# Attention stage rewritten as one uniform body of 16 units, with the score mask added on TensorE and one maximum per unit

## What is computed

```python
qkv = ln(x) @ qkv_w + qkv_b                 # 16 heads of 16
dist = q_pos[:, None] - k_pos[None, :]
allowed = (dist > 0) & (dist <= 128) & (k_pos >= 0)      # a window of 128 keys
scores = where(allowed, q @ k.T * 0.25, -1e9)
local = softmax(scores) @ v
remote = latent_attention(ln(x)) @ rout_w + rout_b       # 64 pooled latents, 4 heads
gate = sigmoid(local @ gl_w + remote_h @ gr_w)           # per head
mixed = gate * local + (1 - gate) * remote_h
x = x + ln(mixed @ out_w + out_b)                        # then the experts' layer on ln(x)
```

## Time and profile before

| what | value |
|---|---|
| median of 3 runs | 2890.73 us (2880.72 to 2892.46) |
| the profiled execution's own time | 2857.07 us |
| its span, first to last instruction | 2855.3 us |
| PE busy | 2078.1 us, 73% |
| DVE busy | 1371.9 us, 48% |
| ACT busy | 909.4 us, 32% |
| POOL busy | 739.7 us, 26% |
| mean granted TensorE clock | 0.80 of full speed |

### The profile page before, as it was taken

The page is one execution under the profiler, slowest core; times in us unless marked ns, Lnnn a source line. Parts: engine busy times, 40 slices in busy tenths (PEclk is TensorE's granted clock), DMA queues, the critical chain, the costliest instruction groups (busy, mean ns, idle before and its releaser), DMA issues. The chain is left out here.

```text
span 2855.3 us, 45682 instructions
## 1 busy us (share of the span) xinstructions
PE 2078.1 (73%) x12978; PEld 1583.8 (55%) x12979; DVE 1371.9 (48%) x3448; ACT 909.4 (32%) x2071; POOL 739.7 (26%) x934
## 2 busy tenths in 40 slices
PE   2777776777677776777674999999879999996000
PEld 1344444444444444444452788788669999996000
DVE  3464555545564556545553444444533333333557
ACT  1323332233323332233322333333234444443001
POOL 1222333223322333223322333423300000001762
PEclk9667766777677766777676999999989999998555
DMA  3233422343144423343132322222212222223564
GB/s 61 43 54 60 74 50 48 58 66 66 38 59 59 74 45 50 54 74 61 36 52 78 103 83 73 91 77 76 77 60 67 68 67 68 68 68 120 154 202 156
DMA packets 180103, 209.74 MB, mean 73 GB/s; under 512 B 28337, under 2 KB 146482, under 8 KB 180066
## 3 DMA queue, kind: packets, MB, share of 16 engines
q1 hardware_dynamic: 167346, 174.54, 27.8%
q0 software_dynamic: 12720, 34.75, 3.7%
HBM read 88.99 MB, written 69.34 MB: 55 GB/s over the span
## 5 line engine op out<-in xcount | busy, mean ns | idle before, releaser
L489 ACT ACTIVATE prob<-bank 128x512 f32<-128x512 f32 (+1 forms) x512 | 251.1, 544 | 484.1 <-PE bank L948 482.8
L924 PE MATMUL bank<-kS,qS 48*128 48x256 f32 (+1 forms) x1024 | 179.6, 444 | 221.2 <-DVE row_max L715 221.2
L399 POOL TENSOR_SCALAR_AFFINE_SELECT prob<-prob 128x512 f32<-128x512 f32 x256 | 164.9, 644 | 672.6 <-ACT prob L489 670.9
L2020 POOL DMA_INDIRECT f_y<-yg_scratch,index x128 | 125.8, 983 | 622.8 <-DVE index L2058 578.5
L924 PEld LDWEIGHTS bank<-kS,qS 48*128 48x128 f32 x1024 | 116.0, 279 | 305.6 <-DVE row_max L715 283.0
L1827 DVE TENSOR_TENSOR b_h<-b_silu,bank 128x352 f32<-128x352 f32 x136 | 70.9, 521 | 336.8 <-ACT b_silu L1779 336.8
L963 PE MATMUL bank<-prob,v_sb 128*32 128x256 f32 (+1 forms) x2048 | 214.5, 506 | 0.0
L1353 POOL DMA_INDIRECT xg_scratch<-rows,pos x128 | 130.1, 1016 | 317.2 <-DVE pos L1508 281.2
L1881 PE MATMUL bank<-wgu_h,bxT_h 128*128 x544 | 191.2, 351 | 15.1 <-DVE bxT_l L1822 6.7
L712 DVE COPY_PREDICATED bank<-from_prev,bank 128x512 f32<-128x512 int32 x192 | 133.4, 695 | 141.0 <-PE bank L924 137.3
L715 DVE TENSOR_REDUCE row_max<-bank 128x4 f32<-128x512 f32 x256 | 176.9, 691 | 44.4 <-PE bank L924 35.0
(11 more groups left out here) (311 smaller groups left out, 5139.0 us busy)
## 6 DMA issues: line engine op xcount, KB each, us to landing
bx<-xg_scratch SPq DMA_DIRECT2D x136, 128.0 KB, 2.0
yg_scratch<-b_y SPq DMA_DIRECT2D x136, 128.0 KB, 1.7
kS<-qk_h SPq DMA_DIRECT2D x128, 128.0 KB, 5.9
qS<-qk_h SPq DMA_DIRECT2D x128, 128.0 KB, 8.0
x_in<-in_L_attn_x_dram SPq DMA_DIRECT2D x16, 512.0 KB, 3.5
kS<-qk_l SPq DMA_DIRECT2D x64, 128.0 KB, 6.8
qS<-qk_l SPq DMA_DIRECT2D x64, 128.0 KB, 8.9
x_res<-in_L_attn_x_dram SPq DMA_DIRECT2D x16, 512.0 KB, 3.5
```

Of the source, the lines that this page charges most:

```text
L399: op = e.affine_select(out=own, in_=own, compare_op=ALU.is_gt, fill=0.0, base=0, pattern=[[0, HG], [1, P]], channel_multiplier=-1)
L489: e.activation(prob[:, u % SLOTS, 2 * hp:2 * hp + 2, 0:w], src[:, :, 0:w], ACT.Exp, scale=SCALE).then_inc(keyed.frees[hp], 1)
L924: op = e.matmul(SB[:, par, hh * WIN + lo:(hh + 1) * WIN], qS[rows, tile, b * P:(b + 1) * P], kS[rows, tile, k0:k0 + w], start=(b > 0), sto ...
```

## The change

It replaces `mid` and `seam` on every engine by one `body(i, buf)` of 16 units, run for i from -2 to 17 (`live` leaves out what lies outside the 16 sequences), two bodies a loop turn:

- `window` and `maxima` still run 7 units ahead, but go on into the next sequence, so that every unit of the body has one. `weigh_values` runs three units behind across the border. `kS`, `qS` and `v_sb` get two buffers.
- Each other piece has a unit: projections of sequence i+1 in units 0 to 8, the turning, gating and mixing of i-1 in units 3 to 13, its output projection in 14 and 15, the input of i+2 in 2 to 14, the residual of i-2 in 0 to 13.
- The mask goes in by matmuls with the identity in every unit (`mask_window`, two of 512 columns); `window` adds the scores onto it. The predicated copy is gone, and the reduction runs over 1024 columns (L825), 512 in block 0.
- The banks: `PV` has one bank (4), bank 5 joins 6 and 7 (`Rounds` counts their uses).
- Local and remote outputs are copied to SBUF by ACT (`keep_local`, `keep_remote`); the gate runs once for four blocks. Two layer norms' scaling moves from DVE to ACT (`normed`; DVE makes the small `shifts`).
- `qk_h` and `qk_l` hold half of the heads: the second half waits for the DMAs of the first. ACT issues the DMA of the maxima itself, after its own write.

The diff, cut to its core, indentation shortened:

```diff
-        PV = ctx.enter_context(nc.psum_tensor("bank45", [P, 2, 512], f32))
-        banks = [t[:, k, :] for t in (SB, KB, PV) for k in range(2)]
-        psum = banks + [ctx.enter_context(nc.psum_tensor(f"bank{b}", [P, 512], f32)) for b in range(6, 8)]
+        banks = [t[:, k, :] for t in (SB, KB) for k in range(2)]
+        psum = banks + [ctx.enter_context(nc.psum_tensor(f"bank{b}", [P, 512], f32)) for b in range(4, 8)]
...
+kS = sb("kS", [P, 2, HEADS // 2, S], f32r)
+qS = sb("qS", [P, 2, HEADS // 2, S], f32r)
+v_sb = sb("v_sb", [P, 2, T, HEADS, PAD])
...
+uses = [["k0", "v0", "v2", "r1", "r2", "k1", "lT0", "xT1", "mix1", "out1"],
+        ["q0", "v1", "r0", "v3", "r3", "q1", "xT0", "mix0", "out0", "ls1"],
+        ["m1", "rkv", "a0", "a1", "m2", "a2", "a3", "rq", "m3", "lT1", "lo", "m0", "ls0"]]
+stage = {name: 1 for names in uses for name in names}
+stage.update({name: 0 for name in ("xT0", "xT1")})
+stage.update({name: 2 for name in ("m1", "m2", "m3", "lT0", "lT1", "lo")})
+stage.update({f"{kind}{n}": 3 for kind, count in (("a", T), ("r", T), ("mix", 2), ("out", 2)) for n in range(count)})
+front = Rounds(uses, stage, SEQS, [sem(f"front_full{b}") for b in range(3)], [sem(f"front_free{b}") for b in range(3)])
+FB = [psum[6], psum[7], psum[5]]
+PV = psum[4]
...
+        def body(i, buf):
+            if live(i + 2):
+                load_x(i + 2)
+            if live(i + 1):
+                spread_heads(i + 1, 1 - buf, 0)
+            if live(i - 2):
+                store_x1(i - 2)
+            if live(i + 1):
+                spread_heads(i + 1, 1 - buf, 1)
+            if live(i - 2):
+                store_xn2(i - 2)
+            if live(i - 1):
+                load_residual(i - 1)
...
+        def minus_max(i, buf, g):
             act.wait_ge(*front.filled(i, f"m{g}"))
             act.wait_ge(max_placed[g], 16 * i)
             e.activation(maxT[:, g, :], FB[front.bank(f"m{g}")][0:HG * T, 0:P], ACT.Copy,
                          scale=-1.0).then_inc(front.free(f"m{g}"), 1)
+            act.wait_ge(*front.read(i, f"m{g}"))
+            act.dma_start(qS[TERMS:P:PAIR, buf, 2 * g:2 * g + 2, :].bitcast(f32), maxT[:, g, :].bitcast(f32)).then_inc(max_placed[g], 16)
...
+        def normed(k, i, tile, ts):
+
+            act.wait_ge(shift_known[k // 2], i + 1)
+            if k == 2:
+                act.wait_ge(stored, 32 * i + 16)
+            for t in ts:
+                op = e.activation(tile[:, t, :], tile[:, t, :], ACT.Identity, scale=rstd[:, k, t:t + 1],
+                                  bias=shift[:, k // 2, t:t + 1])
+            if ts[-1] == T - 1:
+                op.then_inc((xn_ready, xn2_ready)[k // 2], 1)
...
-            own, prev = (SB[:, :, :].rearrange("p a (t w) -> p (a t) w", t=2)[:, :, k * P:(k + 1) * P] for k in (1, 0))
-            if b == 0:
-                dve.wait_ge(score_full, UNITS * i + u + 1)
-            else:
-                wait_alone(score_full, UNITS * i + u + 1)
-                e.copy_predicated(out=own, mask=from_prev[:, :].bitcast(i32).unsqueeze(1).to_broadcast([P, HG, P]), data=prev
-                                  ).then_inc(score_merged, 1)
-                dve.wait_ge(score_merged, MERGED * i + g * (T - 1) + b)
-            e.tensor_reduce(row_max[:, g, :, b], own, AX.X, ALU.max).then_inc(score_free, 1)
+            lo = P if b == 0 else 0
+            dve.wait_ge(score_full, UNITS * i + u + 1)
+            e.tensor_reduce(row_max[:, g, :, b], SB[:, :, :].rearrange("p a (t w) -> p (a t) w", t=2)[:, :, lo:WIN],
+                            AX.X, ALU.max).then_inc(score_free, 1)
...
+        def window(i, buf, u):
 
             g, b = units[u]
             if b == 0 and g % 2 == 0:
                 pe.wait_ge(spread[g // 2], SPREAD * (i + 1))
             pe.wait_ge(score_free, UNITS * i + u)
-            if b == 0:
-                for par in range(2):
-                    own = SB[:, par, :].rearrange("p (t w) -> p t w", t=2)[:, :, P:WIN]
-                    e.matmul(own, ident_r[:, :], mask_first[:, :].unsqueeze(1).to_broadcast([P, 2, P]),
-                             start=True, stop=False, skip_group_check=True)
             lo, w = (P, P) if b == 0 else (0, WIN)
+            mask = (mask_first if b == 0 else mask_window)[:, :].unsqueeze(1).to_broadcast([P, 2, w])
+            for par in range(2):
+                e.matmul(SB[:, par, :].rearrange("p (t w) -> p t w", t=2)[:, :, lo:WIN], ident_r[:, :], mask,
+                         start=True, stop=False, skip_group_check=True)
             k0 = max(b - 1, 0) * P
             for hh in range(2):
                 for par in range(2):
                     rows, tile = slice(par * PAIR, par * PAIR + TERMS), 2 * g + hh
-                    op = e.matmul(SB[:, par, hh * WIN + lo:(hh + 1) * WIN], qS[rows, tile, b * P:(b + 1) * P],
-                                  kS[rows, tile, k0:k0 + w], start=(b > 0), stop=True, skip_group_check=True)
+                    op = e.matmul(SB[:, par, hh * WIN + lo:(hh + 1) * WIN], qS[rows, buf, tile, b * P:(b + 1) * P],
+                                  kS[rows, buf, tile, k0:k0 + w], start=False, stop=True, skip_group_check=True)
             op.then_inc(score_full, 1)
...
-                pe.wait_ge(pv_read, G * i + max(g - 1, 0))
-                if g < 2:
-                    pe.wait_ge(pv_used, 2 * i)
+                pe.wait_ge(pv_read, G * i + g)
             for h in range(HG):
-                op = e.matmul(PV[h * PAD:(h + 1) * PAD, g % 2, b * P:b * P + w], v_sb[:, b, g * HG + h, :],
+                op = e.matmul(PV[h * PAD:(h + 1) * PAD, b * P:b * P + w], v_sb[:, buf, b, g * HG + h, :],
                               prob[:, u % SLOTS, 2 * (h % 2) + h // 2, 0:w], start=(b == 0), stop=(b == T - 1),
                               skip_group_check=True)
             op.then_inc(prob_used, 1)
 
...
+        def body(i, buf):
+            prev, nxt, after = i - 1, i + 1, i + 2
+            for u in range(UNITS):
+                if u + AHEAD < UNITS:
+                    if live(i):
+                        window(i, buf, u + AHEAD)
+                elif live(nxt):
+                    window(nxt, 1 - buf, u + AHEAD - UNITS)
+                if live(i):
+                    keyed_scores(i, buf, u)
+                if u >= LAG:
+                    if live(i):
+                        weigh_values(i, buf, u - LAG)
+                elif live(prev):
+                    weigh_values(prev, 1 - buf, UNITS + u - LAG)
+                if u == 0 and live(nxt):
+                    project(nxt, 1, 0)
+                if u == 1:
+                    if live(i):
+                        turn_max(i, 1)
+                    if live(nxt):
+                        project(nxt, 0, 0)
+                if u == 2 and live(nxt):
+                    values(nxt, 0)
+                    latent_pool(nxt)
+                if u == 3:
+                    if live(nxt):
+                        values(nxt, 1)
+                        values(nxt, 2)
+                    if live(prev):
+                        turn_local(prev, 0)
+                        remote(prev, 0)
+                if u == 4:
+                    if live(prev):
+                        turn_local(prev, 1)
+                        remote(prev, 1)
+                    if live(nxt):
+                        values(nxt, 3)
+                if u == 5:
+                    if live(i):
+                        turn_max(i, 2)
+                    if live(prev):
+                        turn_local(prev, 2)
+                        remote(prev, 2)
+                if u == 6:
+                    if live(prev):
+                        turn_local(prev, 3)
+                        remote(prev, 3)
+                    if live(nxt):
+                        latent_queries(nxt)
+                if u == 7 and live(nxt):
+                    project(nxt, 1, 1)
+                if u == 8 and live(nxt):
+                    project(nxt, 0, 1)
+                if u == 9 and live(i):
+                    turn_max(i, 3)
+                    turn_latents(i, 0)
+                if u == 10:
+                    if live(i):
+                        turn_latents(i, 1)
+                    if live(after):
+                        turn_x(after, 0)
+                        turn_x(after, 1)
+                if u == 11 and live(i):
+                    latent_values(i)
+                if u in (12, 13) and live(prev):
+                    turn_mix(prev, u - 12)
+                if u == 13 and live(nxt):
+                    turn_max(nxt, 0)
+                if u in (14, 15):
+                    if live(prev):
+                        project_out(prev, u - 14)
+                    if live(nxt):
+                        latent_scores(nxt, u - 14)
...
```

(41 more changed lines are left out.)

965 lines of the change are left out of this document (471 added, 494 removed).

## The result

| | before | changed |
|---|---|---|
| median of 4 runs each, us | 2887.25 | 2406.62 (2396.80 to 2411.76) |
| ratio, with its 95% interval | | 0.8332 [0.8297, 0.8367] |
| profiled execution, us | 2857.07 | 2411.76 |
| start of routing (first matmul with `ws_h`), us | 1576.9 | 1103.7 |
| from there to the end, us | 1278.4 | 1306.3 |

The kernel is 17% faster.

A forecast was written before the change was run, and what follows sets the result against it. It took the order of copy, maximum and window on one buffer as the bound. PE work of 56 us, 13% idle and clock 0.9 gave a 71 us period, 318 us saved, median 2573 us, range 2450 to 2765.

The forecast's parts named there:

- The bound: Attention loop: copy, maximum and window share one buffer, so their order sets the pace; scores wait 14.1 us for the maximum.
- The sum: Attention period from PE work, idle share and clock: 71 us, a gain of 318 us over 15 repetitions, median 2573 us.
- idle share of 13%: PE's idle part of the new body, taken from the old kernel's dense stretch: 3.72 of 28.90 us.
- clock of 0.9: Granted PE clock in the new body, from the old dense stretch's 0.91: 20% of time at 1.2 GHz.
- the first row: Old kernel's stretch while the seam projects: PE busy 25.18 of 28.90 us, clock 0.91.
- my own equation: Body period P from PE work of 56 us: 0.87P = 56 + 0.088P, giving P = 71.6.
- rival 1: Clock falls in light units 9, 12 and 13: period 80 us, 2708 us, up to 2783; chance 0.20.
- My own list of waits: Added PE waits in the body: DMAs nothing, value bank 0 to 0.2 us, about five bank waits up to 1 us each.
- rival 2: Every wait in the body is covered: period near 61 us, 2423 us; chance 0.10.
- The ends: Filling and draining of attention hold the same chains: 0 change, within 20 us either way.
- The mask part: Identity matmuls in the windows: 12 x 0.56 = 6.7 us of PE work a sequence at full clock, relieving VectorE of copies.

The follow-up runs named there:

- two maxima: The changed kernel with every maximum taken twice on VectorE, the extra one into a tile nobody reads; 2412.68 us, 0.8583 of the kernel before.
- the doubled mask: The changed kernel with each mask matmul pair issued twice, same result; 2397.57 us, 0.8530 of the kernel before.
- three maxima: The changed kernel with every maximum taken three times on VectorE; 2643.54 us, 0.9409 of the kernel before.
- the burst: The changed kernel with the next sequence's first seven windows and maxima together at the end of unit 15, not spread; 2654.63 us, 0.9449 of the kernel before.
- e2_copy: The changed kernel with predicated copy and 512-column maximum in place of the mask matmuls, except in block 0; 2366.67 us, 0.8197 of the kernel before.
- e9_pe_unrolled: The changed kernel with the loop written out on PE alone, other engines keeping theirs; 2292.26 us, 0.8159 of the kernel before.

## Why the prediction was wrong

**The bound, the places and the signs were right.** The order was the bound; with windows between other work the maximum no longer holds PE up. The mask pair (0.56 us), the wide maximum (1.22 for 1.20), VectorE (42.8 for 40.5), ScalarE (36.4 for 37 to 39), GpSimd (27.1 for 26.5) and PE's own work at full clock came out as priced: 54.65 busy for a forecast of 56. No wait of PE in the body exceeds 1.2 us (one of 0.9, for GpSimd's mixing, was not on the list), and the DMAs pin nothing. So the sum of work was right within 3%, and the period forecast was still 12 us too long (71 for a mean of 59.3).

**The step that failed is the choice of the two numbers in "The sum": an idle share of 13% and a clock of 0.9, both from the first row.** In the body inside a turn PE is idle 3.1 of 57.76 us, 5.4%, and the clock is 1.00. By my own equation, either number alone accounts for half: with 13% idle at full clock P = 56/0.87 = 64.4; with 5.4% idle at clock 0.9, 0.946P = 56 + 0.088P gives 65.3; with both as measured, 59.2.

**The clock of 0.91 was a ramp and not a state.** The row was cut at 413.1, where the seam begins at half clock. Cut finer, the same stretch of the kernel before reads:

```profile
413.10:416.00 2.90, 2.90 (x11) 1.83 (x7) 0.00 (x0) 0.06 (x1) 0.55 (x1) 0.50 0.00 0
416.00:419.00 3.00, 3.00 (x15) 1.60 (x14) 0.75 (x1) 0.69 (x1) 0.00 (x0) 0.66 0.20 55
419.00:442.00 23.00, 19.28 (x134) 15.98 (x134) 10.26 (x27) 7.31 (x16) 3.72 (x4) 1.00 1.08 129
```

The level is 0.50 for the first three microseconds, changes in the next three, and is 1.00 for 23 us, with PE idle 16% of them. The mean of the three is 0.91, a value that no part has. The trace held this before the prediction. It shows a dense mixture that kept the full clock with 16% idle, and should have set the term to 1.00. The repeating body inside a turn has no such ramp in it. The Trainium skill, "TensorE: Matmul & The Clock Gate", section "A second HAM failure mode: psum-queue depth-cycling", on which rival 1 leaned, describes a clock that swings by short idles between groups. The bodies of the change, of two maxima and of the doubled mask show none of it (1.00). Those of three maxima and of the burst do (0.89 and 0.85), where PE stands for up to 2.2 us ahead of window after window, and so do some of the predicated copy (0.91 with 4.7 us idle). So the trace agrees for other orders of the work, and for this one it does not: units 9, 12 and 13 do not lower the clock. That the change would stay at 1.00 could not be known from the rows: `e2_copy`, idle 2 us more a body, does not always.

**The idle share was a guess by likeness.** In the seam's 28.9 us, PE waited for ScalarE and VectorE in a chain of one block's gating and turning, each step next to the one it needs (3.7 us of named waits, 3.72 idle). The body puts each such step a unit or more after its source. My own list of waits came to 5.2 us at most a body (0.2, about five times up to 1, and nothing for the DMAs), and I did not use it: adding it to 56 gives 61 at most, the number of rival 2. Measured are 3.1 us. The list had one reading wrong without effect: the 8.9 us of the earlier trace rows is the median landing, not the worst.

**Not foreseen: the pause at the loop's jump**, about 9.5 us five times, 48 us in all. I had said that the loop has two bodies a turn and costed nothing for it. The two errors partly cancel: without it the time would have been about 42 us lower still, as `e9_pe_unrolled` shows.

**The ends** were put at 0, within 20 us. The fifteen periods fell by 493.2 us (1382.8 to 889.6) and the start of routing by 473.2, so filling and draining took 20 us more, at the edge of it: the first `bank<-wrv,pool` comes 6 us sooner, the drain behind the last is 26 longer. The split depends on where a period is cut. From first window to first window the periods fell by 482.6, which leaves 9 us for the ends.

**The mask part** I had told as a cost of 12 x 0.56 us on PE against VectorE's relief, without its sum: I never asked whether it belonged in the change. It does not: it takes 40 us by `e2_copy`, and 50 with the bodies written out.

Summed from the profiled 2857: forecast -318 for attention; measured -493 in the periods (-541 without the pauses, +48 for them), +20 at the ends, +28 behind attention, in sum -445.

## What to carry to other kernels

Cut a stretch again before taking a clock from it, since a mean between two levels can be a ramp that the new code has not, and where the remaining waits are listed and priced one by one, add that list rather than a share from elsewhere. A chain through one buffer that stands alone costs twice, as waiting and as the clock that it lowers for the work around it; between other work it cost PE no wait here. Work moved to the engine that then becomes the bound is a loss even where it relieves another, and a long looped body on PE is worth trying written out.

## What the runs showed of the hardware, unexpected

- At the jump of a loop of two bodies, about 900 matmuls, PE stood still 6 to 8 us without a wait, and worked at half clock after it: 8.4 us for each jump by `e9_pe_unrolled`, 11.4 with four bodies in a turn. The kernel before with two sequences in a turn stood still 3.1 to 3.5 us at each jump, with one sequence not at all. Written out code of the same length, fetched in about as many packets (66 for 80), has no such pause. That the jump's target must first be fetched anew is the likely reading, since the packets rose from 18 to 76 with the longer turn; no run separates it from another cost of the jump.
- The clock stayed at 1.00 through bodies with waits of up to 1.2 us here and there, and fell to 0.89 and 0.85 where PE was idle 12 to 13 us a body in twelve to fourteen waits of up to 2.2 us. The kernel before held 1.00 for 23 us with 3.7 us of idle time in them. Two bodies of `e2_copy` with the same instructions ran at 1.00 and 0.91 with 5.2 and 4.7 us idle.
- The stretch behind the last matmul, which gathers the experts' rows, took 239 us at up to 209 GB/s in one profile of the changed kernel and 195 us at up to 279 GB/s in the other. That is 44 of the 75 us by which the same code differed behind attention (1306 and 1231). Why it differed is open.
